# The mask add moved from TensorE to VectorE's maxima in two attentions, and the latent attention's order of projection, values' product and rope changed

## The reference

```python
x = x + mla(layernorm(x), L0 weights)        # 16 heads, latent queries (192) and keys (64 + 64 rope)
x = x + ternary(layernorm(x))
x = x + gated_delta(layernorm(x))
x = x + ternary(layernorm(x))
x = x + mla(layernorm(x), L1 weights)
x = x + ffn(layernorm(x))                    # with a small attention (16 heads of 16) that modulates the gate
x = x + rotary_attention(layernorm(x))       # 16 heads of 16
x = x + ffn(layernorm(x))
```

```python
scores = jnp.where(causal, jnp.einsum('bhqd,bhkd->bhqk', query, key) * scale, -inf)
probs = jax.nn.softmax(scores, axis=-1)
out = jnp.einsum('bhqk,bhkd->bhqd', probs, v)
```

## Time and profile before

| | us |
|---|---|
| median of 3 runs | 3569.63 |
| lowest, highest run | 3565.03, 3569.97 |
| span of the profiled execution | 3572.4 |
| TensorE, VectorE, ScalarE, GpSimd busy | 3322.9, 2352.9, 1912.1, 817.2 |
| mean granted TensorE clock | 0.976 of full speed |

### The profile page before, as it was taken

One profiled execution on the slowest core, in us unless ns is written; L12 is line 12 of the kernel. 1 busy time (PEld: TensorE's weight loads), 2 busy tenths in 40 slices (PEclk: granted clock), 3 DMA queues, 4 the chain that ended last, 5 costly groups with the idle time before them and its releaser, 6 DMA issues. The chain is left out here.

```text
span 3572.4 us, 88785 instructions
## 1 busy us (share of the span) xinstructions
PE 3322.9 (93%) x34858; PEld 2714.8 (76%) x34858; DVE 2352.9 (66%) x6069; ACT 1912.1 (54%) x4767; POOL 817.2 (23%) x828
## 2 busy tenths in 40 slices
PE   6999986999999999999999789999789999999999
PEld 5777765888888888888888667777667777777787
DVE  4666655778787878787877546666545666666654
ACT  3554544666666666666666435545445454544543
POOL 2232321222222222222222223233200111111100
PEclk9999998999999999999999989999989999999999
DMA  6000000000000000000000030000000000000000
GB/s 224 1 1 1 1 1 22 17 23 17 23 17 20 20 20 20 20 19 15 20 20 20 26 133 1 1 1 1 1 1 1 1 1 1 1 4 4 4 7 10
DMA packets 51330, 66.69 MB, mean 19 GB/s; under 512 B 4962, under 2 KB 40291, under 8 KB 49379
## 3 DMA queue, kind: packets, MB, share of 16 engines
q1 hardware_dynamic: 50914, 61.00, 5.4%
HBM read 58.43 MB, written 2.56 MB: 17 GB/s over the span
## 5 line engine op out<-in xcount | busy, mean ns | idle before, releaser
L1285 DVE SCALAR_TENSOR_TENSOR d_acc<-d_raw,d_taps,d_acc 128x255 f32<-128x255 f32 (+2 forms) x1152 | 642.8, 599 | 146.7 <-ACT d_raw L1275 133.1
L2358 ACT ACTIVATE s_probs<-bank,s_nmax 128x128 f32<-128x128 f32 (+1 forms) x768 | 249.4, 436 | 369.9 <-DVE s_nmax L2350 369.9
L1510 ACT COPY d_power<-bank 128x768 f32<-128x768 f32 x320 | 259.0, 810 | 217.1 <-PE bank L1503 217.1
L1273 ACT ACTIVATE d_acc<-bank,d_tap_bias,d_taps 128x256 f32<-128x256 f32 x384 | 196.0, 561 | 167.1 <-PE bank L1254 160.6
L2350 DVE TENSOR_REDUCE s_nmax<-bank 128x4 f32<-128x512 f32 x192 | 174.7, 952 | 96.9 <-PE bank L2340 96.7
L698 POOL TENSOR_TENSOR a_q<-a_rope 64x512 f32<-64x512 f32 x128 | 163.3, 1276 | 279.4 <-DVE a_rope L688 238.3
L2381 DVE COPY s_probsT<-bank 128x384 f32<-128x384 f32 x192 | 106.8, 556 | 167.2 <-PE bank L2367 163.4
L738 ACT ACTIVATE a_area<-bank,a_nmax 128x128 f32<-128x128 f32 x256 | 93.7, 366 | 175.9 <-DVE a_nmax L729 175.7
L688 DVE TENSOR_TENSOR a_rope<-bank,a_sinT 32x512 f32<-32x512 f32 x256 | 177.4, 693 | 5.7
L183 POOL TENSOR_TENSOR rstd<-var_eps,minus_half 128x2 f32<-128x2 f32 x64 | 46.0, 718 | 585.5 <-DVE var_eps L165 449.3
L765 ACT COPY a_area<-bank 128x512 f32<-128x512 f32 (+1 forms) x260 | 138.4, 580 | 73.4 <-PE bank L756 72.0
(11 more groups left out here) (275 smaller groups left out, 9000.0 us busy)
## 6 DMA issues: line engine op xcount, KB each, us to landing
d_alpha<-d_alpha_rows SPq DMA_DIRECT2D x64, 256.0 KB, 3.5
d_g_decay<-d_running_rows SPq DMA_DIRECT2D x32, 258.0 KB, 3.4
a_w_o<-in_a_w_o SPq DMA_DIRECT2D x2, 2048.0 KB, 16.6
a_area<-in_a_q_nope SPq DMA_DIRECT2D x2, 1536.0 KB, 8.2
x<-in_x SPq DMA_DIRECT2D x8, 256.0 KB, 16.2
d_wk<-in_d_wk SPq DMA_DIRECT2D x1, 2048.0 KB
d_wq<-in_d_wq SPq DMA_DIRECT2D x1, 2048.0 KB
d_wv<-in_d_wv SPq DMA_DIRECT2D x1, 2048.0 KB
```

The lines of the kernel that those rows point to most:

```text
L1273: nc.scalar.activation(acc[:, r % 3, j], b_proj[:, j * T:(j + 1) * T], ACT.Identity, scale=taps[:, r // 2, h, 3:4], bias=tap_bias[:, r // ...
L1285: last = nc.vector.scalar_tensor_tensor(out=acc[:, r % 3, j, d:T], in0=raw[:, r % 2, j, 0:T - d], scalar=taps[:, r // 2, h, 3 - d:4 - d], ...
L1510: nc.scalar.copy(power[:], b_step[:, :, 0:3 * P]).then_inc(g.step_out, 1)
L2358: last = nc.scalar.activation(probs[:, s % 2, i, cols], heads[:, i, cols], ACT.Exp, bias=nmax[:, s % 2, t, i:i + 1])
```

## The change

In both attentions the mask matmuls go. The mask is kept in SBUF in float32 as 384 columns (mask, zeros, mask). VectorE's reductions are replaced by an instruction that writes -(scores + mask) to the probabilities' tile and their minimum, which is the negated maximum, to `nmax`; the exponential is then taken in place in SBUF with scale -1. In latent attention `scores_pe` waits for the maxima of the head before last in the bank, not for its exponentials, and the wait for the probabilities' buffer moves from ScalarE to VectorE. In the stream there are eight such instructions a slot in place of two reductions, head by head, and ScalarE waits for each. In latent attention TensorE takes `project_pe(n+2)` ahead of `pv_pe(n-1)`; VectorE takes the maxima, then `oT_dve`, then `rope_dve(n+2)`, ahead of all steps of the next batch and of the reciprocal; GpSimd takes `rope_pool(n+2)` ahead of its other steps.

```diff
+def masked_max_dve(core, out, scores, blocks, nmax):
+    return core.nc.vector.tensor_tensor_reduce(
+        out=out, in0=scores, in1=core.mask[:, blocks], scale=-1.0, scalar=HIGHEST, op0=ALU.add,
+        op1=ALU.min, accum_out=nmax)
...
         def scores_pe(pe, n, j):
-            pe.wait_ge(*g.probs_ready(0, h - 1))
+            pe.wait_ge(*g.max_ready(0, h - 1))
             out = b_s[j]
-            nc.tensor.matmul(out[:, 0:P], q[:, n % 2, j, 0:P], keys[:, 0:P], start=True, stop=False,
+            nc.tensor.matmul(out[:, 0:P], q[:, n % 2, j, 0:P], keys[:, 0:P], start=True, stop=True,
                              skip_group_check=True)
-            nc.tensor.matmul(out[:, P:3 * P], q[:, n % 2, j, P:T], keys, start=False, stop=False,
-                             skip_group_check=True)
-            diagonal = out[:, :].rearrange("p (b k) -> p b k", b=4)[:, 0:3:2]
-            nc.tensor.matmul(diagonal, core.ident_bf[:], core.mask_bf[:, :].rearrange(
-                "p (b k) -> p b k", b=2), start=False, stop=True,
-                skip_group_check=True).then_inc(g.scores_in_psum.sem, 1)
+            nc.tensor.matmul(out[:, P:3 * P], q[:, n % 2, j, P:T], keys, start=False, stop=True,
+                             skip_group_check=True).then_inc(g.scores_in_psum.sem, 1)
         def max_dve(dve, n, j):
-            dve.wait_ge(*g.probs_ready(0, h + 1 - AHEAD))
-            nc.vector.tensor_reduce(nmax[:, h % AHEAD, 0:1], b_s[j][:, 0:P], AX.X, ALU.max,
-                                    negate=True)
-            nc.vector.tensor_reduce(nmax[:, h % AHEAD, 1:2], b_s[j][:, P:3 * P], AX.X, ALU.max,
-                                    negate=True).then_inc(g.max_ready.sem, 1)
+            dve.wait_ge(*g.probsT_in_psum(0, h + 1 - AHEAD))
+            for t, cols in enumerate((slice(0, P), slice(P, 3 * P))):
+                last = masked_max_dve(core, probs[:, h % AHEAD, cols], b_s[j][:, cols], cols,
+                                      nmax[:, h % AHEAD, t:t + 1])
+            last.then_inc(g.max_ready.sem, 1)
         def exp_act(act, n, j):
-            act.wait_ge(*g.probsT_in_psum(0, h + 1 - AHEAD))
...
+                own = probs[:, h % AHEAD, cols]
+                last = nc.scalar.activation(own, own, ACT.Exp, scale=-1.0, ...
@@ TensorE's loop, latent attention
+                    if n + 2 < PAIRS_ALL:
+                        project_pe(pe, n + 2)
                     if 0 < n <= PAIRS_ALL:
                         pv_pe(pe, n - 1)
-                    if n + 2 < PAIRS_ALL:
-                        project_pe(pe, n + 2)
@@ VectorE's loop
-                    if n > 1:
-                        oT_dve(dve, n - 2)
                     if n < PAIRS_ALL:
                         max_dve(dve, n, 0)
                         max_dve(dve, n, 1)
+                    if n > 1:
+                        oT_dve(dve, n - 2)
+                    if n + 2 < PAIRS_ALL:
+                        rope_dve(dve, n + 2)
...
                     if n < PAIRS_ALL:
                         recip_dve(dve, n)
-                    if n + 2 < PAIRS_ALL:
-                        rope_dve(dve, n + 2)
@@ GpSimd's loop
                     pool.wait_ge(*g.q_rope_ready(0, min(n + 2, PAIRS_ALL)))
+                    if n + 2 < PAIRS_ALL:
+                        rope_pool(pool, n + 2)
+                        pool.wait_ge(*g.q_rope_ready(0, n + 3))
...
                     spread_pool(pool, n)
-                    if n + 2 < PAIRS_ALL:
-                        pool.wait_ge(*g.recip_spread(0, n + 1))
-                        rope_pool(pool, n + 2)
+                    pool.wait_ge(*g.recip_spread(0, n + 1))
@@ the stream
         def scores_pe(pe, s):
-            for i in range(GS):
-                nc.tensor.matmul(heads[:, i].rearrange("p (b k) -> p b k", b=4)[:, 0:3:2],
-                                 core.ident_bf[:], core.mask_bf[:, :].rearrange(
-                                     "p (b k) -> p b k", b=2), start=True, stop=False,
-                                 skip_group_check=True)
...
         def max_dve(dve, s):
             need(dve, g.scores_in_psum, s + 1)
-            need(dve, g.probs_ready, GS * (s - 1))
-            for t, cols in ((0, slice(0, P)), (1, slice(P, 3 * P))):
-                nc.vector.tensor_reduce(nmax[:, s % 2, t], heads[:, :, cols], AX.X, ALU.max,
-                                        negate=True).then_inc(g.max_ready, 1)
+            need(dve, g.probsT_in_psum, GS * (s - 1))
+            for i in range(GS):
+                for t, cols in ((0, slice(0, P)), (1, slice(P, 3 * P))):
+                    masked_max_dve(core, probs[:, s % 2, i, cols], heads[:, i, cols], cols,
+                                   nmax[:, s % 2, t, i:i + 1]).then_inc(g.max_ready, 1)
         def exp_act(act, s):
-            need(act, g.probsT_in_psum, GS * (s - 1))
-            need(act, g.max_ready, 2 * (s + 1))
-            for t, cols in ((0, slice(0, P)), (1, slice(P, 3 * P))):
-                for i in range(GS):
-                    last = nc.scalar.activation(probs[:, s % 2, i, cols], heads[:, i, cols], ACT.Exp,
+            for i in range(GS):
+                for t, cols in ((0, slice(0, P)), (1, slice(P, 3 * P))):
+                    need(act, g.max_ready, 2 * (GS * s + i) + t + 1)
+                    own = probs[:, s % 2, i, cols]
+                    last = nc.scalar.activation(own, own, ACT.Exp, scale=-1.0,
                                                 bias=nmax[:, s % 2, t, i:i + 1])
```

More of the change, by code:

```diff
@@ L18 @@
 MASKED = -1.0e30
+HIGHEST = 3.0e38
 class Signal:
@@ L48, in __init__ @@
         self.nc, self.ins, self.ctx = nc, ins, ctx
-        self.x = sb("x", [P, NB + 1, NT, D])
+        self.x = sb("x", [P, NB, NT, D])
         self.ident = sb("ident", [P, P])
         self.ident_bf = sb("ident_bf", [P, P], BF16)
-        self.mask_bf = sb("mask_bf", [P, 2 * P], BF16)
-        self.mask_f = sb("mask_f", [P, P])
+        self.mask = sb("mask", [P, 3 * P])
         self.minus_half = sb("minus_half", [P, 16])
@@ L124, in _ @@
             sp.dma_start(core.ident[:], ins["ident"][:]).then_inc(core.ready, 16)
-            sp.dma_start(core.mask_f[:], ins["mask"][:]).then_inc(core.ready, 16)
+            sp.dma_start(core.mask[:], ins["mask"][:]).then_inc(core.ready, 16)
         @block.vector
@@ L133, in _ @@
             nc.vector.tensor_copy(core.ident_bf[:], core.ident[:])
-            nc.vector.tensor_copy(core.mask_bf[:, 0:P], core.mask_f[:])
-            nc.vector.tensor_copy(core.mask_bf[:, P:2 * P], core.mask_f[:])
         @block.gpsimd
@@ L139, in _ @@
             core.ln_rstd.prime(pool, 1)
-            nc.gpsimd.memset(core.x[:, NB], 0.0)
             nc.gpsimd.memset(core.minus_half[:], -0.5)
@@ L2340, in scores_pe @@
                     last = nc.tensor.matmul(heads[:, i, cols], qm[rows, j % 2, k // 2, k % 2, tok],
-                                            qk[rows, j % 2, k // 2, 1, 0:keys], start=False,
-                                            stop=True, tile_position=(32 * i, 0),
+                                            qk[rows, j % 2, k // 2, 1, 0:keys],
+                                            start=(cols.start == 0), stop=True, tile_position=(32 * i, 0),
                                             skip_group_check=True)
@@ L2680, in layout @@
     f["ident"] = np.eye(P, dtype=np.float32)
-    f["mask"] = np.triu(np.full((P, P), MASKED, np.float32), 1)
+    f["mask"] = np.zeros((P, 3, P), np.float32)
+    f["mask"][:, 0::2] = np.triu(np.full((P, P), MASKED, np.float32), 1)[:, None]
+    f["mask"] = f["mask"].reshape(P, 3 * P)
     def mla(tag, qa, qln, qb, ckv, kpe, kvln, kvb, wo):
```

13 lines of the change are left out of this document (6 added, 7 removed).

## The result

The changed kernel takes 3612.35 us (median of 4, 3609.97 to 3624.72); the kernel before takes 3569.8 us. The ratio is 1.0124, with a 95% interval of 1.0106 to 1.0142: slower by 43 us, where 3574 us were forecast and 3610 was the end of the range. The profiled execution has a span of 3608.2 us against 3572.4.

A forecast was written before the change was run, and what follows sets the result against it. TensorE, busy 93% of the span, was taken to bound the kernel. Latent attention +9.7 us and stream -5.6 us gave +4 us on the 3569.6 us median: 3574 us, range 3537 to 3610.

The forecast's parts named there:

- step 5: Latent attention, rope moved ahead of other work: second pair +21, sixth pair's wait +33, clock +24, seventh pair -6 and -22.
- Step 1: Both attentions: each removed mask matmul frees 0.107 us of TensorE, -27.4 us in latent attention and -41.1 in the stream.
- Step 2: Stream, VectorE: masked maxima with an accumulator read of 0.07 us each take 2.8 us per slot instead of 1.74.
- rival B: VectorE's maxima: the accumulator read costs nothing, 2.2 us per slot, total 3537 us; chance 0.17.
- Step 3: Stream: slots wait for later maxima (+31.5, +6.4, +8.5, +2.1), earlier exponentials give -13; with the masks -5.6 us.
- Step 4: Latent attention: TensorE's waits at the values' product in the fourth and fifth pair fall behind the projection, -12.9 us.
- Step 5, second pair: Latent attention: normalized x comes later behind rope, a new TensorE wait of 1.5 us, +21 us over 14.
- Step 5, fifth and sixth pair: Latent attention: VectorE's norm waits for GpSimd, TensorE waits 4.0 us in the sixth pair: +33 us, and +24 for the clock.
- Step 5, seventh pair: Latent attention: the wait for the second normalization falls from 2.12 to 1.65 us, -6 us, and the clock stays up, -22.
- rival C: Clock still falls at the seventh pair's wait (+22) and in seven modulation slots of the stream (+12): 3608 us; chance 0.23.
- E: Latent attention: the sixth pair does not wait longer, so +33 and +24 fall away: 3517 us, half of it 3545; chance 0.17.
- D: VectorE's maxima: the accumulator read costs ScalarE's 0.20 us, +65 us in slots and pairs, 3639 us; chance 0.10.

The follow-up runs named there:

- e7: e4 with one more VectorE instruction, a 128x384 addition, behind the maxima in each stream slot: 3462.72 us.
- e9: e4 with TensorE's values' product ahead of the projection again, as before the change: 3661.19 us.
- e5: The changed kernel with GpSimd's rope addition waiting for normalized x in the second and seventh pair, VectorE's order kept: 3538.09 us.
- e2: The changed kernel with VectorE's normalization ahead of its rope products in the second and seventh pair: 3504.61 us.
- e3: The changed kernel with GpSimd's latent preparation ahead of its rope addition, and VectorE's mean squares ahead of its rope products, in the fifth pair: 3523.43 us.
- e4: The changed kernel with the moves of e2 and e3 together: 3431.26 us.
- e1: The changed kernel with the old order of TensorE, VectorE and GpSimd in latent attention, mask still in VectorE's maxima: 3527.17 us.

## Why the prediction was wrong

The likeliest case was no change, +4 us; +43 were measured. Two large errors, +69 in latent attention and its surroundings and -37 in the stream, hid each other in part. Nearly all of the +69 lies in two terms of step 5, by the pairs of both calls with the masks' 0.21 us per pair set apart: the second and third pair cost 57 us where 21 were forecast, and the seventh and eighth 4 where a gain of 28 was. The sixth pair (55 against 57) and the fourth and fifth (-16 against -13) came as forecast.

- **Step 1, the masks.** The mask matmuls are gone, and where nothing else is late the pair is 0.23 us shorter (6.00 to 5.77), as two times 0.107 says. Right.
- **Step 2, the maxima: mis-sized.** 2.22 us per slot, not 2.8. The row that I took for the accumulator read was the distance between two tiny instructions; the read overlaps the next instruction and costs nothing. The value was rival B's, at 0.17. The Trainium skill (VectorE: DVE Perf Modes, "Two Vector instructions with no wait between them") says that there are two instructions, and the trace agrees, with an 83 ns row for each; that a second instruction takes time of its own was my addition, and the trace is against it.
- **Step 3, the stream: right in kind.** -43 us instead of -5.6. Nearly all of the error is step 2's: with e7's 2.69 us the gain is 9.8 us. That this comes so near is in part luck, since two errors of step 3 offset each other: e7 shows more slots that pay (67 against 48), and the slots without steps gained more than forecast. There are 11, and they gained 25 us, 5 of them the masks, where 13 were forecast beside the masks: five in which the clock had fallen before gained 2.3 to 3.8 us each, and the six with the clock at 1.00 before and after 1.6 to 1.8.
- **Step 4, TensorE's order: right, and under-priced as a need.** The fourth and fifth pair are 0.83 and 0.73 us shorter, 0.2 of each the masks, so 1.1 us per batch against the 0.92 forecast. e9 shows that without it every pair would wait 1.16 us or more.
- **Step 5, second pair: the step that failed.** The place was right, the 1.5 us were 2.07, because the normalization runs beside GpSimd's rope addition and takes 1.68 us instead of the 0.75 of the sum. And I asked for the clock only behind the sixth and seventh pair's waits; behind this one it falls too, in 11 of the 12 batches with a wait of 2.07 us. The second and third pair cost 2.8 + 0.8 us per batch in the first call and 2.7 + 1.0 in the second, +51 us over 14, where +21 was forecast. With the masks' 6 us added back 36 us were missing in the sum. The longer waits are some 12 of them (0.57 us in 12 batches, and 4.23 and 3.89 us in the first batch of each call instead of 1.5); the rest goes with the clock. e5 and e2 show both parts.
- **Step 5, fifth and sixth pair: right.** VectorE waits 3.81 us for GpSimd and TensorE 3.62, against 3.6 to 4.4 forecast, and the clock falls. The pair costs 3.4 us more in the first call and 4.1 in the second, +52 us against 57 forecast. The even 1.7 us per batch for the clock was right only as a mean: against the 10.99 us without a fall it cost nothing, 1.3 or 3.0 us in the batches of the first call. e3 takes it away. The forecast of its undoing was too small, since e3's order is better than that of before and not only equal to it.
- **Step 5, seventh pair: wrong.** 28 us of gain were forecast, from a wait of 1.65 instead of 2.12 us. It is 2.14 us, for the same reason as in the second pair (e5 brings it to 1.19), and the clock falls as it did before, in 9 of 11 batches: this is rival C's place, and its direction was right.
- **Rivals.** C gave 3608 us and the measured time is 3612; that is luck, by other amounts. B's cheap maxima came, worth -37 us, and with C's +34 that makes 3571; most of the rest is the second pair. Of the seven modulation slots in which C had the clock fall, it fell in two. E and D are excluded by the 3.81 us wait and by the 83 ns read that delays nothing.

The Trainium skill has the rule for step 5's miss (SBUF — State Buffer, "SBUF: two separate sides"): GpSimd and a VectorE instruction that needs both of VectorE's ports to SBUF, or reads two inputs from SBUF, share one pair of ports; the one that starts first has it for its whole length, and the other stands still. The trace agrees. In the changed kernel each of the 25 normalizing instructions that start while L702 runs takes 1.35 us instead of 0.41 and ends 0.15 us behind L702; in e4 the 14 norms of L571 that do so take 1.30 us instead of 0.28 and end 0.08 us behind it. The 26 normalizing instructions that had started ahead of L702 keep their 0.38 to 0.41 us. The sum of step 5 priced no such overlap. The row was in the trace of before as well, where L567 took 1.29 us beside the rope addition in 14 of 32 cases, and I had used it only as an upper bound.

Open: why the clock falls behind one wait and not behind another of the same length, and why e1's plain pairs gain 0.13 us and not the 0.21 of their masks. Neither was tried. The 3.1 us more between the two latent attentions were not followed.

## What to carry to other kernels

Before an operation is moved ahead of another on a queue, ask of each engine which later consumer is nearest: here rope's result was needed a whole pair later and the normalization 2 us later, and putting the urgent one first, here and for the latent preparation, was worth 181 us, four times what the change lost. Look at what runs at the same time on VectorE and GpSimd, not only at each queue; a GpSimd instruction nobody waits for can stretch the VectorE instruction that everybody waits for. And when a weight load is late, read the load's own row: the matmul's wait row hides most of it.

## What the runs showed of the hardware that was not expected

- VectorE's accumulator read (83 ns in its row) starts together with the next instruction. The masked maxima take 0.21 and 0.35 us from start to start for 128 and 256 columns; 0.35 is also what the plain two-input instruction took in the earlier trace rows. Beside a GpSimd instruction (101 of the 512 in latent attention) they stay at 0.29 and 0.42 us; they read one input from PSUM and one from SBUF.
- Beside GpSimd's 64x512 addition two 128x256 normalizations take 1.68 us instead of 0.73, and one 128x64 norm 1.30 instead of 0.28; GpSimd's addition is itself 1.31 to 1.42 us instead of 1.27. Only the VectorE instruction that starts while the addition runs is stretched.
- The granted clock stayed at its upper level behind all 24 waits of 1.12 to 1.19 us for normalized x in e5. In the changed kernel it fell behind 11 of 12 waits of 2.07 us and was down behind 12 of the 14 of 3.62 to 3.90 us at the sixth pair's values' product. At 1.9 us both are common in one kernel (e1, down in 8 of 14): two sixth pairs, with waits of 1.89 and 1.90 us, and in the 3.6 us behind them 1.00 in one and 0.63 in the other.

```profile
147.00:150.60 3.60, 3.60 (x22) 2.87 (x18) 2.01 (x8) 2.44 (x9) 0.00 (x0) 1.00 0.00 0
206.40:210.00 3.60, 3.60 (x15) 2.83 (x12) 0.88 (x7) 1.90 (x9) 0.00 (x0) 0.63 0.02 5
```
